# Linear attention: softmaxes of one batch beside the transposes and products of the batch in front of it

## The chip, the cores and the metric

The kernel runs on one NeuronCore of one Trainium2 chip. The metric is the device time of one execution in microseconds (us), as the median of several runs. TensorE (PE) does the matrix products and the transposes, VectorE (DVE) and ScalarE (ACT) work elementwise, GpSimd (POOL) has no work in the stage in question, and the queue of SyncE (SP) issues the DMAs. The engines run apart from each other and wait for each other on semaphores only. Each engine executes its own instructions in the order in which they are written.

## The reference

The program runs four layers on an input of 4 batches x 1024 rows x 512 columns: softmax attention, linear attention, and two state space layers. The change touches the linear attention alone, which is this part of the second layer (16 heads of 32 columns; `mask` hides key rows):

```
    k = jnp.where(mask, -jnp.inf, k)
    v = jnp.where(mask, 0.0, v)
    ...
    q = jax.nn.softmax(q, axis=-1)          # over the 32 columns of a head
    k = jax.nn.softmax(k, axis=2)           # over the 1024 rows of a batch
    attn = jnp.einsum('bhse,bhsd->bhed', k, v)
    y = jnp.einsum('bhtd,bhed->bhte', q, attn)
```

The projections before it have written k transposed (`kT`), q, and v (already masked) to device memory. The stage writes `y` back there, and the next projection reads it.

## The kernel before

`linear_attention` is one block between two barriers. For each of the 4 batches it loads 2 MB of `kT`, 0.5 MB of mask, 2 MB of `q` and 2 MB of `v`, all on SP's queue, and then does these steps. The lines are those of the kernel before.

- **Key softmax.** DVE makes the additive mask `mneg` (L946). Four times, once for each 128 columns, DVE adds it to `kT`, writes `ks` and takes the extreme `nmax` (L950), and ACT takes the exponential with a running sum (L980). DVE inverts the sums (L958) and scales `ks` (L961).
- **Query softmax.** DVE takes the maximum of each head `qmax` (L954) and subtracts it (L956), ACT takes the exponential of all of `q` (L983), DVE sums (L964), inverts (L966) and scales (L968).
- **Turning.** PE transposes the keys into 8 PSUM banks (L1001, "k turn" here), and ACT copies them to `kn` (L986). PE transposes the queries into the same 8 banks (L1008, "q turn"), and ACT copies them to `qT` (L989).
- **Products.** PE multiplies `kn` with `v` into bank 0 (L1013, the "at" product); DVE copies the diagonal 32x32 blocks to `at` (L972, four copies of 32 partitions); PE multiplies `qT` with `at` into the 8 banks (L1019, the "y" product); ACT copies them to `y` (L993); SP stores `y` (L924).

DVE, ACT, PE and SP each run a hardware loop over the batches with these steps in that order. There is one buffer of each of `kT`, `ks`, `q`, `v`. All loads count on one semaphore, `kv_in`, and DVE's first instruction of a batch (L946) waits for all four loads of that batch. SP loads the next `kT` when the four L950 are done, the next `q` when the q turn is done, and the next `v` when the at product is done. On DVE the copy to `at` is the last step of a batch, so the masks and maxima of the next batch stand behind it.

Of the kernel before, what the change touches and what calls it, by code (L numbers as in the profile page):

```python
# [19 lines left out]
P = 128  # L20
# [856 lines left out]

def linear_attention(core, ident, io, scr):

    nc = core.nc  # L880
    with ExitStack() as ctx:
        sb, psum = allocator(nc, ctx, "lin")
        kT = sb("kT", [P, KT, T])
        q = sb("q", [P, TT, D])
        v = sb("v", [P, TT, D])
        mi = sb("mi", [P, T], I32)
        mneg = sb("mneg", [P, T])
        ks = sb("ks", [P, KT, T])
        nmax = sb("nmax", [P, KT])
        ksum = sb("ksum", [P, KT])  # L890
        kr = sb("kr", [P, KT])
        kn = sb("kn", [P, TT, D])
        qmax = sb("qmax", [P, TT * H])
        qsum = sb("qsum", [P, TT * H])
        qr = sb("qr", [P, TT * H])
        qT = sb("qT", [P, KT, T])
        at = sb("at", [P, KT, P])
        y = sb("y", [P, TT, D])
        banks = [psum(f"bank{k}", [P, HALF]) for k in range(8)]
        kv_in = core.count("kv_in")  # L900
        chain_v, y_stored = core.vector_step, core.turned_out[0]
        lin = {n: core.count("lin_" + n) for n in ("k_shift", "k_exp", "k_norm", "q_shift", "q_exp", "q_norm",
                                                   "k_turn", "k_copy", "q_turn", "q_copy", "at", "at_copy",
                                                   "y", "y_copy")}
# [3 lines left out]
        @block.sync  # L908
        def _(sp):
            rows = lambda name, b: scr[name][b].rearrange("(k p) d -> p k d", p=P)  # L910

            def load_k(b):
                sp.dma_start(kT[:], scr["kT"][b]).then_inc(kv_in.handle, 16)
                sp.dma_start(mi[:], io["mask1"][bass.ds(b, 1), :].broadcast_to([P, T])).then_inc(kv_in.handle, 16)

            def load_q(b):
                sp.dma_start(q[:], rows("q", b)).then_inc(kv_in.handle, 16)

            def load_v(b):
                sp.dma_start(v[:], rows("v", b)).then_inc(kv_in.handle, 16)  # L920

            def store_y(b):
                w(sp, "y_copy", b * TT + TT)
                sp.dma_start(scr["y"][b].rearrange("(k p) d -> p k d", p=P), y[:]).then_inc(y_stored.handle, 16)  # L924

            load_k(0)
            load_q(0)
            load_v(0)
            with sp.Fori(0, B - 1) as b:

                w(sp, "k_shift", b * KT + KT)
                load_k(b + 1)
                w(sp, "q_turn", b * TT + TT)
                load_q(b + 1)
                w(sp, "at", b + 1)
                load_v(b + 1)
                store_y(b)
            store_y(B - 1)
            sp.wait_ge(y_stored.handle, y_stored.at(B * 16))

        @block.vector
        def _(dve):
            nc.vector.memset(at[:], 0.0)
            with dve.Fori(0, B) as b:
# [3 lines left out]
                core.apart(dve)  # L948
                for kt in range(KT):
                    nc.vector.tensor_tensor_reduce(ks[:, kt], kT[:, kt], mneg[:], -1.0, HUGE, ALU.add, ALU.min,  # L950
                                                   nmax[:, kt:kt + 1]).then_inc(lin["k_shift"].handle, 1)
                qv = q[:].rearrange("p k (h e) -> p (k h) e", e=DH)
                wide = lambda x: x[:].unsqueeze(2).broadcast_to([P, TT * H, DH])
                nc.vector.tensor_reduce(qmax[:], qv, AX.X, ALU.max).then_inc(chain_v.handle, 1)  # L954
                dve.wait_ge(chain_v.handle, chain_v.at(b * 4 + 2))
                nc.vector.tensor_tensor(qv, qv, wide(qmax), ALU.subtract).then_inc(lin["q_shift"].handle, 1)  # L956
                w(dve, "k_exp", b * KT + KT)
                nc.vector.reciprocal(kr[:], ksum[:]).then_inc(chain_v.handle, 1)  # L958
                dve.wait_ge(chain_v.handle, chain_v.at(b * 4 + 3))
                for kt in range(KT):  # L960
                    last = nc.vector.tensor_scalar(ks[:, kt], ks[:, kt], kr[:, kt:kt + 1], None, ALU.mult)  # L961
# [4 lines left out]
                nc.vector.reciprocal(qr[:], qsum[:]).then_inc(lin["q_norm"].handle, 1)  # L966
                w(dve, "q_norm", b * 2 + 1)
                nc.vector.tensor_tensor(qv, qv, wide(qr), ALU.mult).then_inc(lin["q_norm"].handle, 1)  # L968
                w(dve, "at", b + 1)
                for g in range(4):  # L970
                    r = slice(32 * g, 32 * g + 32)
                    last = nc.vector.tensor_copy(at[r, :, r], banks[0][:].rearrange("p (k e) -> p k e", e=P)[r, :, r])  # L972
                last.then_inc(lin["at_copy"].handle, 1)

        @block.scalar
        def _(act):
            with act.Fori(0, B) as b:
                for kt in range(KT):
                    w(act, "k_shift", b * KT + (kt + 1))
                    nc.scalar.activation(ks[:, kt], ks[:, kt], ACT.Exp, bias=nmax[:, kt:kt + 1], scale=-1.0,  # L980
                                         accum_out=ksum[:, kt:kt + 1]).then_inc(lin["k_exp"].handle, 1)
                w(act, "q_shift", b + 1)
                nc.scalar.activation(q[:], q[:], ACT.Exp).then_inc(lin["q_exp"].handle, 1)  # L983
                for t in range(TT):
                    w(act, "k_turn", b * TT + (t + 1))
                    nc.scalar.copy(kn[:, t], banks[t][:]).then_inc(lin["k_copy"].handle, 1)  # L986
                for t in range(TT):
                    w(act, "q_turn", b * TT + (t + 1))
                    nc.scalar.copy(qT[:, t % 4, (t // 4) * HALF:(t // 4 + 1) * HALF], banks[t][:]).then_inc(lin["q_copy"].handle, 1)  # L989
                act.wait_ge(y_stored.handle, y_stored.at(b * 16))  # L990
                for t in range(TT):
                    w(act, "y", b * TT + (t + 1))
                    nc.scalar.copy(y[:, t], banks[t][:]).then_inc(lin["y_copy"].handle, 1)  # L993

        @block.tensor
        def _(pe):
            with pe.Fori(0, B) as b:
                w(pe, "k_norm", b + 1)
                for t in range(TT):
                    for kt in range(KT):  # L1000
                        last = nc.tensor.transpose(banks[t][:, kt * P:(kt + 1) * P], ks[:, kt, t * P:(t + 1) * P], ident[:])  # L1001
                    last.then_inc(lin["k_turn"].handle, 1)
                w(pe, "q_norm", b * 2 + 2)
                w(pe, "k_copy", b * TT + TT)
                for o in range(8):
                    h, kt = o // 4, o % 4
                    for z in range(4):
                        last = nc.tensor.transpose(banks[o][:, z * P:(z + 1) * P], q[:, h * 4 + z, kt * P:(kt + 1) * P], ident[:])  # L1008
                    last.then_inc(lin["q_turn"].handle, 1)
                w(pe, "q_copy", b * TT + TT)  # L1010
                for kt in range(KT):
                    for t in range(TT):
                        last = nc.tensor.matmul(banks[0][:, kt * P:(kt + 1) * P], v[:, t, kt * P:(kt + 1) * P],  # L1013
                                                kn[:, t, kt * P:(kt + 1) * P], start=(t == 0), stop=(t == TT - 1))
                last.then_inc(lin["at"].handle, 1)
                w(pe, "at_copy", b + 1)
                for t in range(TT):
# [5 lines left out]
    kv_in.stage_added(64 * B)  # L1023
# [943 lines left out]
```

## Time and profile before

| what | value |
|---|---|
| median of 3 runs | 7153.99 us (7148.65 to 7154.7) |
| the profiled execution | 7149.81 us |
| its span in the trace | 7147.8 us |
| the linear attention stage in it | first load issued at 2441.51 us, last copy to `y` starts at 2667.78 us |
| one batch in it (start of L946 to the next) | 50.58, 51.04 and 50.85 us |

The trace counts time from the start of the span. A row of the timeline gives the start, the duration, the engine, the line, the operation with output and inputs, how many instructions were merged into the row, and in brackets how long the engine was idle before it and who ended that.
### The profile page before, as it was taken

The page shows a single profiled execution, that of the slowest core. Times are in us where ns is not written, and L with a number is a line of the kernel's source. Part 1 is how long each engine was busy: PE and PEld are TensorE (multiplying, and loading weights), DVE is VectorE, ACT ScalarE, POOL GpSimd, SP SyncE.
Part 4 walks back from the last instruction along what each step waited for, and adds up shares of the span by engine and source line. Part 5 has one row for each costly group of instructions (what it writes and reads, how often), then busy time and mean ns, then how long its engine had stood idle before and what let it go on. Part 6 is the DMA issues. An engine that isn't in the chain of part 4 may idle for free. (4 is left out here: it accounts for less than half of the span.)

```text
span 7147.8 us, 89203 instructions
## 1 busy us (share of the span) xinstructions
PE 5974.3 (84%) x31488; PEld 4032.9 (56%) x31488; DVE 5020.6 (70%) x6369; ACT 4535.2 (63%) x6817; POOL 2482.0 (35%) x1098
## 2 busy tenths in 40 slices
PE   6989999999889757988858888886888768888883
PEld 2448888888634353434356666663344356666662
DVE  2459999999742245454489999994444489999992
ACT  1228888888621142444478999993455489999991
POOL 0000000000000000000079999993000089999993
PEclk9999999999989878999889999998999899999996
DMA  5442222222242244233356665653233456655554
GB/s 196 170 151 60 72 63 72 67 73 60 79 156 97 107 149 179 86 140 131 149 149 158 172 160 159 158 156 102 97 140 121 153 153 162 159 153 155 154 146 169
DMA packets 608855, 935.18 MB, mean 131 GB/s; under 512 B 104984, under 2 KB 252568, under 8 KB 607908
## 3 DMA queue, kind: packets, MB, share of 16 engines
q1 hardware_dynamic: 596964, 904.27, 41.9%
q0 software_dynamic: 5120, 16.78, 0.7%
q10 hardware_dynamic: 6336, 8.52, 0.3%
q8 instruction: 249, 4.08, 0.3%
q14 instruction: 186, 1.52, 0.1%
HBM read 590.40 MB, written 338.98 MB: 130 GB/s over the span
## 5 line engine op out<-in xcount | busy, mean ns | idle before, releaser
L1609 POOL TENSOR_TENSOR scan_hC<-scan_h,scan_Crep 128x1024 f32<-128x1024 f32 x1024 | 2395.2, 2378 | 2866.5 <-DVE scan_h L1776 2839.1
L1720 ACT ACTIVATE scan_a<-scan_dt,scan_A 128x512 f32<-128x512 f32 x2048 | 1368.2, 697 | 89.9 <-DVE scan_h L1776 72.7
L1643 PE MATMUL scan_y<-ident,scan_hC 128*128 128x128 f32 x8192 | 1114.1, 279 | 298.8 <-POOL scan_hC L1609 293.2
L1643 PEld LDWEIGHTS scan_y<-ident,scan_hC 128*128 128x128 f32 x8192 | 903.5, 142 | 687.6 <-POOL scan_hC L1609 639.7
L1776 DVE TENSOR_TENSOR_SCAN scan_h<-scan_a,scan_carry,scan_h 128x512 f32<-128x512 f32 x1024 | 1217.1, 1261 | 21.9 <-ACT scan_a L1720 19.4
L1776 DVE TENSOR_TENSOR_SCAN scan_h<-scan_a,scan_h 128x512 f32<-128x512 f32 x1024 | 1155.3, 1200 | 55.3 <-ACT scan_a L1720 54.9
L1696 ACT COPY scan_h<-scan_drive 128x1024 f32<-128x1024 f32 x1024 | 1041.8, 1017 | 168.9 <-PE scan_drive L1631 157.2
L1631 PE MATMUL scan_drive<-scan_Bd,scan_dT 128*128 128x256 f32 x4096 | 750.8, 305 | 129.9 <-ACT scan_h L1696 79.3
L805 DVE TENSOR_TENSOR att_pTlo<-att_TP,att_pThi 128x512 fp32r<-128x512 f32 x1024 | 658.1, 684 | 128.0 <-ACT att_pThi L843 126.6
L843 ACT CAST att_pThi<-att_TP 128x512 fp32r<-128x512 f32 x1024 | 547.3, 586 | 180.3 <-PE att_TP L738 173.0
L1631 PEld LDWEIGHTS scan_drive<-scan_Bd,scan_dT 128*128 128x128 f32 x4096 | 558.6, 192 | 181.9 <-issue 96.3
L798 DVE CUSTOM_DVE_ANT_0 att_sm<-att_S,att_mneg 128x1024 f32<-128x1024 f32 x512 | 622.1, 1215 | 12.1 <-POOL att_mneg L716 11.9
L858 ACT ACTIVATE att_pr<-att_sm,att_nmax 128x1024 f32<-128x1024 f32 x512 | 593.0, 1158 | 45.7 <-DVE att_nmax L798 45.7
L738 PE MATMUL att_TP<-ident,att_pr 128*128 128x128 f32 x4096 | 565.4, 278 | 25.6 <-DVE att_pTlo L805 25.6
L497 PE MATMUL p_bank<-p_W,p_xT 128*128 128x512 f32 x1280 | 565.0, 597 | 5.3 <-ACT p_xT L395 5.3
L738 PEld LDWEIGHTS att_TP<-ident,att_pr 128*128 128x128 f32 x4096 | 452.2, 141 | 185.0 <-issue 116.0
L746 PE MATMUL att_YT<-att_pThi,att_v 128*64 128x256 f32 x2048 | 538.3, 298 | 0.0
L1669 PE MATMUL scan_O<-scan_Wo,scan_gT 128*128 128x512 f32 x1024 | 531.9, 613 | 5.4 <-ACT scan_gT L1727 5.4
L1205 PE MATMUL ssmin_ring<-ssmin_Wz,ssmin_xT 128*128 128x512 f32 x1024 | 476.9, 614 | 46.9 <-ACT ssmin_zt L1275 46.9
L746 PE MATMUL att_YT<-att_pTlo,att_v 128*64 128x256 f32 x2048 | 496.7, 277 | 0.0
L716 POOL TENSOR_SCALAR att_mneg<-att_mrow 128x1024 f32<-128x1024 f32 x4 | 14.5, 3635 | 1268.0 <-DMA att_mrow<-mask 840.3
L1205 PE MATMUL ssmin_ring<-ssmin_xT,ssmin_Wx 128*128 128x512 f32 x1024 | 453.1, 598 | 0.0
(151 smaller groups left out, 6826.8 us busy)
## 6 DMA issues: line engine op xcount, KB each, us to landing
scan_dT<-scratch_dtuT SPq DMA_DIRECT2D x512, 256.0 KB, 5.5
scratch_dtuT<-ssmin_dT SPq DMA_DIRECT2D x128, 512.0 KB, 2.9
scan_Crep<-scratch_bc SPq DMA_DIRECT2D x64, 1024.0 KB, 9.7
att_q<-scratch_q_split SPq DMA_DIRECT2D x256, 128.0 KB, 3.0
att_k<-scratch_k_split SPq DMA_DIRECT2D x256, 128.0 KB, 3.2
scratch_uD<-ssmin_uD SPq DMA_DIRECT2D x64, 512.0 KB, 4.4
scratch_z<-ssmin_zt SPq DMA_DIRECT2D x128, 256.0 KB, 2.0
scratch_dt<-ssmin_dt SPq DMA_DIRECT2D x64, 512.0 KB, 2.6
```

The costliest lines, as they stand in the source:

```text
L738: last = nc.tensor.transpose(TP[:, m * P:(m + 1) * P], pr[u % 2][:, m * P:(m + 1) * P], ident[:])
L746: last = nc.tensor.matmul(YT[:, pair * 2 % 4:pair * 2 % 4 + 2, :], v[n // 4 % 2][:, m, n % 4, :].bitcast(F32R), pT[part][pair % 2][:, :, m ...
L798: nc.vector.tensor_tensor_reduce(sm[u % 2][:], S[u % 2][:], mneg[b % 2][:], -1.0, HUGE, ALU.add, ALU.min, nmax[u % 2][:]).then_inc(s["shif ...
L805: nc.vector.tensor_tensor(pT[1][u // 2 % 2][:, u % 2, cols_].bitcast(F32R), TP[:, cols_], pT[0][u // 2 % 2][:, u % 2, cols_], ALU.subtract ...
L858: nc.scalar.activation(pr[u % 2][:], sm[u % 2][:], ACT.Exp, bias=nmax[u % 2][:, 0:1], scale=-1.0, accum_out=psums[:, at:at + 1]).then_inc( ...
L1205: last = nc.tensor.matmul(ring[e % 4][:], lhs, rhs, start=(kt == 0), stop=(kt == KT - 1))
L1609: nc.gpsimd.tensor_tensor(hC[k % 2][:], of, Crep[:, 2 * p:2 * p + 2, :], ALU.mult).then_inc(s["scaled"].handle, 1)
L1631: last = nc.tensor.matmul(drive[:, c * TC:(c + 1) * TC, :], dT[j][:, at * P:(at + 1) * P].bitcast(F32R), Bd[th][:, at, :, first:first + GS ...
L1643: last = nc.tensor.matmul(y[j][:, t, :], hC[k % 2][:, i, t * P:(t + 1) * P], ident[:], start=(p == 0 and i == 0 and t == 0), stop=False, i ...
L1696: nc.scalar.copy(h[group % 3][:, :, tt * P:(tt + 1) * P], drive[:].rearrange("p t n -> p n t")).then_inc(s["laid"].handle, 1)
L1720: nc.scalar.activation(a[(2 * k + i) % 3][:], dt[j][:], ACT.Exp, scale=A[:, m, 2 * p + i:2 * p + i + 1]).then_inc(s["decayed"].handle, 1)
L1776: nc.vector.tensor_tensor_scan(of, a[(2 * k + i) % 3][:], of, first, ALU.mult, ALU.add).then_inc(s["scanned"].handle, 1)
```

## The change

The lines below are those of the changed kernel, about 25 further down.

- `ks`, `q` and `v` get two buffers each, batch b uses number b % 2. `kT`, the mask, `kn`, `qT`, `at`, `y` and the 8 banks stay single.
- The one semaphore for loads becomes several: `k_in` (kT and mask), `q_in` and `v_in` (one for each buffer). DVE waits for `k_in` at the mask and for `q_in` before the maximum of `q`; PE waits for `v_in` before the at product.
- SP issues the loads of batches 0 and 1 first, and in step b those of batch b + 2 ahead of the store of `y`.
- ACT does the exponentials of batch b + 1 between the `qT` copies and the `y` copies of batch b.
- DVE does the copy to `at` of batch b - 1 in batch b, behind the inverse of the sums of `q` and in front of the last scaling of `q`.
- PE keeps its order within a batch. Its waits become one for each bank where it waited for all eight (L1023, L1030), and the at product waits for one copy of `qT` only.
- The hardware loops are gone: the code of the four batches stands in a row. The one `sem_inc` of `core.apart` on DVE is gone too.

```
+            def copy_at(b):
+                w(dve, "at", b + 1)
+                if b >= 1:
+                    w(dve, "y", b * TT)
...
                 nc.vector.reciprocal(qr[:], qsum[:]).then_inc(lin["q_norm"].handle, 1)
+                if b >= 1:
+                    copy_at(b - 1)
                 w(dve, "q_norm", b * 2 + 1)
                 nc.vector.tensor_tensor(qv, qv, wide(qr), ALU.mult).then_inc(lin["q_norm"].handle, 1)
-                w(dve, "at", b + 1)
...
+            copy_at(B - 1)
...
+            exponentials(0)
+            for b in range(B):
...
+                if b + 1 < B:
+                    exponentials(b + 1)
+                if b >= 1:
+                    act.wait_ge(y_stored.handle, y_stored.at(b * 16))
                 for t in range(TT):
                     w(act, "y", b * TT + (t + 1))
...
-                dve.wait_ge(kv_in.handle, kv_in.at(b * 64 + 64))
+                dve.wait_ge(k_in.handle, k_in.at(b * 32 + 32))
...
+                dve.wait_ge(q_in[b % 2].handle, q_in[b % 2].at(b // 2 * 16 + 16))
...
             load_v(0)
-            with sp.Fori(0, B - 1) as b:
...
+            load_k(1)
+            load_q(1)
+            load_v(1)
+            for b in range(B):
+                if b + 2 < B:
+                    load_k(b + 2)
+                    load_q(b + 2)
+                    load_v(b + 2)
```

**ACT's order.** Before, these are the last rows of the loop body on ACT: the copies to `kn`, `qT` and `y`, and the branch back to the exponentials.

```order
L986 COPY lin_kn<-lin_bank 128x512
L989 COPY lin_qT<-lin_bank 128x512 x8
L990 ISA
L993 COPY lin_y<-lin_bank 128x512 x8
L977 REGISTER_ALU
L977 COMPARE_AND_BRANCH
```

Now, from the `kn` copies of batch 0 to the exponential of `q` of batch 2:

```order
L1003 COPY lin_kn<-lin_bank 128x512 x8
L1008 COPY lin_qT<-lin_bank 128x512 x8
L992 ACTIVATE lin_ks,lin_ksum<-lin_ks,lin_nmax 128x1024 x4
L995 ACTIVATE lin_q<-lin_q 128x4096
L1015 COPY lin_y<-lin_bank 128x512 x8
L1003 COPY lin_kn<-lin_bank 128x512 x8
L1008 COPY lin_qT<-lin_bank 128x512 x8
L992 ACTIVATE lin_ks,lin_ksum<-lin_ks,lin_nmax 128x1024 x4
L995 ACTIVATE lin_q<-lin_q 128x4096
```

The exponentials of the next batch (L992, L995) have moved in front of the `y` copies of the batch (L1015), and stand behind its `qT` copies (L1008).

**DVE's order.** Before, the end of the loop body on DVE, from the inverse of the sums of `q`:

```order
L966 RECIPROCAL lin_qr<-lin_qsum 128x128
L905 ISA
L968 TENSOR_TENSOR lin_q<-lin_q,lin_qr 128x4096
L972 COPY lin_at<-lin_bank 32x4x32 x4
L944 REGISTER_ALU
L944 COMPARE_AND_BRANCH
```

Now, the end of batch 1 and the start of batch 2, with the semaphores that each row waits for (`lin_q1` and `lin_ks0` are buffers; `lin_bank0` holds the at product of batch 0):

```order
L975 TENSOR_REDUCE lin_qsum<-lin_q1 128x128 [waits lin_q_exp]
L977 RECIPROCAL lin_qr<-lin_qsum 128x128 [waits vector_step]
L947 COPY lin_at<-lin_bank0 32x4x32 [waits lin_at]
L947 COPY lin_at<-lin_bank0 32x4x32 x3
L981 TENSOR_TENSOR lin_q1<-lin_q1,lin_qr 128x4096 [waits lin_q_norm]
L954 TENSOR_SCALAR lin_mneg<-lin_mi 128x1024 [waits input_in0]
L961 ISA lin_ks0,lin_nmax<-lin_kT,lin_mneg 128x1024 [waits lin_k_exp,lin_k_turn,vector_step]
```

The copy to `at` (L947) is that of the batch in front. It stands behind the whole softmax of the next batch but for the last scaling of `q` (L981).

## Rows read from the trace of the kernel before

**Rows 1.** Busy us (x records) of PE, PEld, DVE, ACT, POOL in the second batch.

```profile
2514.60:2565.50 50.90, 27.44 (x194) 26.55 (x193) 27.89 (x23) 22.07 (x33) 0.00 (x0) 0.73 0.48 175
```

**Rows 2.** Waits in the stage: us in total, times, longest.

```profile
DVE lin_at L972 <- PE lin_bank L1013: 58.1, 4, 14.7
DVE lin_mneg L946 <- DMA lin_v<-scratch_v: 43.7, 4, 21.8
```

**Rows 3.** DMA issues at the stage's head (2441.5 to 2464), us to landing.

```profile
lin_q<-scratch_q SPq DMA_DIRECT2D x1, 2048.0 KB, 16.3
lin_mi<-mask SPq DMA_DIRECT2D x1, 512.0 KB, 10.8
```

**Rows 4.** Timeline of the first batch: start, us, engine, line, operation.

```profile
2441.90 0.42 SPq L914 DMA_DIRECT2D lin_mi<-mask  x1
2442.38 0.43 SPq L917 DMA_DIRECT2D lin_q<-scratch_q  x1
...
2464.01 0.69 DVE L946 TENSOR_SCALAR lin_mneg<-lin_mi 128x1024 f32<-128x1024 int32 x1 [21.84 <-DMA lin_v<-scratch_v]
...
2469.48 4.41 DVE L954 TENSOR_REDUCE lin_qmax<-lin_q 128x128 f32<-128x4096 f32 x1
...
2478.38 3.62 ACT L983 ACTIVATE lin_q<-lin_q 128x4096 f32<-128x4096 f32 x1 [7.55 <-DVE lin_q L956]
2478.47 2.74 DVE L961 TENSOR_SCALAR lin_ks<-lin_ks,lin_kr 128x1024 f32<-128x1024 f32 x4
...
2481.27 6.11 PE L1001 MATMUL lin_bank<-ident,lin_ks 128*128 128x128 f32 x32 [43.52 <-DVE lin_ks L961]
2482.03 4.42 DVE L964 TENSOR_REDUCE lin_qsum<-lin_q 128x128 f32<-128x4096 f32 x1 [0.82 <-ACT lin_q L983]
...
2485.83 2.27 ACT L986 COPY lin_kn<-lin_bank 128x512 f32<-128x512 f32 x4 [0.27 <-PE lin_bank L1001]
2486.49 0.95 DVE L966 RECIPROCAL lin_qr<-lin_qsum 128x128 f32<-128x128 f32 x1
2487.48 4.42 DVE L968 TENSOR_TENSOR lin_q<-lin_q,lin_qr 128x4096 f32<-128x4096 f32 x1
...
2492.03 5.85 PE L1008 MATMUL lin_bank<-ident,lin_q 128*128 128x128 f32 x32 [4.65 <-DVE lin_q L968]
...
2496.59 2.05 ACT L989 COPY lin_qT<-lin_bank 128x512 f32<-128x512 f32 x4 [0.27 <-PE lin_bank L1008]
...
2498.70 7.41 PE L1013 MATMUL lin_bank<-lin_kn,lin_v 128*128 128x128 f32 x64 [0.81 <-ACT lin_qT L989]
...
2506.15 1.19 DVE L972 COPY lin_at<-lin_bank 32x128 f32<-32x128 f32 x4 [14.25 <-PE lin_bank L1013]
...
2507.39 7.41 PE L1019 MATMUL lin_bank<-lin_at,lin_qT 128*128 128x128 f32 x64 [1.28 <-DVE lin_at L972]
```

**Rows 5.** Timeline at later batches: DVE's start of batch 2, ACT's last key exponential, the last copy.

```profile
2514.59 0.69 DVE L946 TENSOR_SCALAR lin_mneg<-lin_mi 128x1024 f32<-128x1024 int32 x1 [7.25 <-DMA lin_v<-scratch_v]
...
2622.07 1.15 ACT L980 ACTIVATE lin_ks<-lin_ks,lin_nmax 128x1024 f32<-128x1024 f32 x1
...
2667.78 0.58 ACT L993 COPY lin_y<-lin_bank 128x512 f32<-128x512 f32 x1 [0.31 <-PE lin_bank L1019]
```

**Rows 6.** Granted clock (behind the busy times) at the k turn, and after the y product.

```profile
2481.27:2486.00 4.73, 4.73 (x22) 4.73 (x23) 3.97 (x1) 3.24 (x6) 0.00 (x0) 0.50 0.00 0
2486.00:2487.40 1.40, 1.38 (x12) 1.14 (x10) 1.36 (x2) 1.28 (x3) 0.00 (x0) 0.92 0.00 0
...
2514.80:2516.80 2.00, 0.00 (x1) 0.00 (x0) 1.81 (x4) 0.65 (x2) 0.00 (x0) 1.00 0.13 49
2516.80:2531.80 15.00, 0.00 (x0) 0.00 (x0) 14.92 (x13) 7.45 (x9) 0.00 (x0) 0.50 0.83 308
```

**Rows 7.** The page's head, and the queue that carries the program's code.

```profile
span 7147.8 us, 89203 instructions
...
q8 instruction: 249, 4.08, 0.3%
```

More of the change, by code:

```diff
@@ L882, in linear_attention @@
         sb, psum = allocator(nc, ctx, "lin")
+        two = lambda n, shape: [sb(f"{n}{j}", shape) for j in range(2)]
         kT = sb("kT", [P, KT, T])
[L884 to L896, printed above, removed]
+        ks, q, v = two("ks", [P, KT, T]), two("q", [P, TT, D]), two("v", [P, TT, D])
+        mi, mneg = sb("mi", [P, T], I32), sb("mneg", [P, T])
+        nmax, ksum, kr = sb("nmax", [P, KT]), sb("ksum", [P, KT]), sb("kr", [P, KT])
+        kn, qT, y = sb("kn", [P, TT, D]), sb("qT", [P, KT, T]), sb("y", [P, TT, D])
+        qmax, qsum, qr = (sb(n, [P, TT * H]) for n in ("qmax", "qsum", "qr"))
         at = sb("at", [P, KT, P])
-        y = sb("y", [P, TT, D])
         banks = [psum(f"bank{k}", [P, HALF]) for k in range(8)]
-        kv_in = core.count("kv_in")
         chain_v, y_stored = core.vector_step, core.turned_out[0]
+        k_in, q_in, v_in = core.input_in[0], core.slot_in[0:2], core.slot_in[2:4]
         lin = {n: core.count("lin_" + n) for n in ("k_shift", "k_exp", "k_norm", "q_shift", "q_exp", "q_norm",
@@ L912, in load_k @@
             def load_k(b):
-                sp.dma_start(kT[:], scr["kT"][b]).then_inc(kv_in.handle, 16)
-                sp.dma_start(mi[:], io["mask1"][bass.ds(b, 1), :].broadcast_to([P, T])).then_inc(kv_in.handle, 16)
+                if b >= 1:
+                    w(sp, "k_shift", b * KT)
+                sp.dma_start(kT[:], scr["kT"][b]).then_inc(k_in.handle, 16)
+                sp.dma_start(mi[:], io["mask1"][b:b + 1, :].broadcast_to([P, T])).then_inc(k_in.handle, 16)
             def load_q(b):
-                sp.dma_start(q[:], rows("q", b)).then_inc(kv_in.handle, 16)
+                if b >= 2:
+                    w(sp, "q_turn", (b - 1) * TT)
+                sp.dma_start(q[b % 2][:], rows("q", b)).then_inc(q_in[b % 2].handle, 16)
             def load_v(b):
[L920 to L924, printed above, removed]
+                if b >= 2:
+                    w(sp, "at", b - 1)
+                sp.dma_start(v[b % 2][:], rows("v", b)).then_inc(v_in[b % 2].handle, 16)
             load_k(0)
@@ L928, in _ @@
             load_v(0)
-            with sp.Fori(0, B - 1) as b:
[L931 to L938, printed above, removed]
+            load_k(1)
[6 more added lines that the diff above has]
+                    load_v(b + 2)
+                w(sp, "y_copy", b * TT + TT)
+                sp.dma_start(scr["y"][b].rearrange("(k p) d -> p k d", p=P), y[:]).then_inc(y_stored.handle, 16)
             sp.wait_ge(y_stored.handle, y_stored.at(B * 16))
@@ L942, in _ @@
         def _(dve):
+            wide = lambda x: x[:].unsqueeze(2).broadcast_to([P, TT * H, DH])
+            def copy_at(b):
+                w(dve, "at", b + 1)
+                if b >= 1:
+                    w(dve, "y", b * TT)
+                for g in range(4):
+                    r = slice(32 * g, 32 * g + 32)
+                    last = nc.vector.tensor_copy(at[r, :, r], banks[0][:].rearrange("p (k e) -> p k e", e=P)[r, :, r])
+                last.then_inc(lin["at_copy"].handle, 1)
             nc.vector.memset(at[:], 0.0)
-            with dve.Fori(0, B) as b:
-                dve.wait_ge(kv_in.handle, kv_in.at(b * 64 + 64))
+            for b in range(B):
+                key, query = ks[b % 2], q[b % 2]
+                dve.wait_ge(k_in.handle, k_in.at(b * 32 + 32))
                 nc.vector.tensor_scalar(mneg[:], mi[:], 1.0, -HUGE, ALU.is_equal, ALU.mult).then_inc(chain_v.handle, 1)
                 dve.wait_ge(chain_v.handle, chain_v.at(b * 4 + 1))
-                core.apart(dve)
+                if b >= 2:
+                    w(dve, "k_turn", (b - 1) * TT)
+                if b >= 1:
+                    w(dve, "k_exp", b * KT)
                 for kt in range(KT):
-                    nc.vector.tensor_tensor_reduce(ks[:, kt], kT[:, kt], mneg[:], -1.0, HUGE, ALU.add, ALU.min,
+                    nc.vector.tensor_tensor_reduce(key[:, kt], kT[:, kt], mneg[:], -1.0, HUGE, ALU.add, ALU.min,
                                                    nmax[:, kt:kt + 1]).then_inc(lin["k_shift"].handle, 1)
-                qv = q[:].rearrange("p k (h e) -> p (k h) e", e=DH)
-                wide = lambda x: x[:].unsqueeze(2).broadcast_to([P, TT * H, DH])
+                qv = query[:].rearrange("p k (h e) -> p (k h) e", e=DH)
+                dve.wait_ge(q_in[b % 2].handle, q_in[b % 2].at(b // 2 * 16 + 16))
                 nc.vector.tensor_reduce(qmax[:], qv, AX.X, ALU.max).then_inc(chain_v.handle, 1)
@@ L960, in _ @@
                 for kt in range(KT):
-                    last = nc.vector.tensor_scalar(ks[:, kt], ks[:, kt], kr[:, kt:kt + 1], None, ALU.mult)
+                    last = nc.vector.tensor_scalar(key[:, kt], key[:, kt], kr[:, kt:kt + 1], None, ALU.mult)
                 last.then_inc(lin["k_norm"].handle, 1)
@@ L966, in _ @@
                 nc.vector.reciprocal(qr[:], qsum[:]).then_inc(lin["q_norm"].handle, 1)
+                if b >= 1:
+                    copy_at(b - 1)
                 w(dve, "q_norm", b * 2 + 1)
                 nc.vector.tensor_tensor(qv, qv, wide(qr), ALU.mult).then_inc(lin["q_norm"].handle, 1)
-                w(dve, "at", b + 1)
-                for g in range(4):
-                    r = slice(32 * g, 32 * g + 32)
-                    last = nc.vector.tensor_copy(at[r, :, r], banks[0][:].rearrange("p (k e) -> p k e", e=P)[r, :, r])
@@ L973, in _, with exponentials @@
-                last.then_inc(lin["at_copy"].handle, 1)
+            copy_at(B - 1)
         @block.scalar
         def _(act):
-            with act.Fori(0, B) as b:
+            def exponentials(b):
+                key, query = ks[b % 2], q[b % 2]
                 for kt in range(KT):
                     w(act, "k_shift", b * KT + (kt + 1))
-                    nc.scalar.activation(ks[:, kt], ks[:, kt], ACT.Exp, bias=nmax[:, kt:kt + 1], scale=-1.0,
+                    if b >= 1 and kt == 0:
+                        w(act, "k_norm", b)
+                    nc.scalar.activation(key[:, kt], key[:, kt], ACT.Exp, bias=nmax[:, kt:kt + 1], scale=-1.0,
@@ L981, in _ @@
                                          accum_out=ksum[:, kt:kt + 1]).then_inc(lin["k_exp"].handle, 1)
                 w(act, "q_shift", b + 1)
-                nc.scalar.activation(q[:], q[:], ACT.Exp).then_inc(lin["q_exp"].handle, 1)
+                nc.scalar.activation(query[:], query[:], ACT.Exp).then_inc(lin["q_exp"].handle, 1)
+            exponentials(0)
+            for b in range(B):
                 for t in range(TT):
                     w(act, "k_turn", b * TT + (t + 1))
+                    if b >= 1 and t == 0:
+                        w(act, "at", b)
@@ L986, in _ @@
                     nc.scalar.copy(kn[:, t], banks[t][:]).then_inc(lin["k_copy"].handle, 1)
[L987 to L990, printed above, removed]
+                for o in range(TT):
+                    w(act, "q_turn", b * TT + (o + 1))
+                    if b >= 1 and o == 0:
+                        w(act, "y", b * TT)
+                    nc.scalar.copy(qT[:, o % 4, (o // 4) * HALF:(o // 4 + 1) * HALF], banks[o][:]).then_inc(lin["q_copy"].handle, 1)
@@ L991, in _ @@
+                if b + 1 < B:
+                    exponentials(b + 1)
+                if b >= 1:
+                    act.wait_ge(y_stored.handle, y_stored.at(b * 16))
                 for t in range(TT):
@@ L996, in _ @@
         def _(pe):
-            with pe.Fori(0, B) as b:
+            for b in range(B):
                 w(pe, "k_norm", b + 1)
                 for t in range(TT):
+                    if b >= 1:
+                        w(pe, "y_copy", (b - 1) * TT + t + 1)
                     for kt in range(KT):
-                        last = nc.tensor.transpose(banks[t][:, kt * P:(kt + 1) * P], ks[:, kt, t * P:(t + 1) * P], ident[:])
+                        last = nc.tensor.transpose(banks[t][:, kt * P:(kt + 1) * P], ks[b % 2][:, kt, t * P:(t + 1) * P], ident[:])
                     last.then_inc(lin["k_turn"].handle, 1)
                 w(pe, "q_norm", b * 2 + 2)
-                w(pe, "k_copy", b * TT + TT)
                 for o in range(8):
                     h, kt = o // 4, o % 4
+                    w(pe, "k_copy", b * TT + o + 1)
                     for z in range(4):
-                        last = nc.tensor.transpose(banks[o][:, z * P:(z + 1) * P], q[:, h * 4 + z, kt * P:(kt + 1) * P], ident[:])
+                        last = nc.tensor.transpose(banks[o][:, z * P:(z + 1) * P], q[b % 2][:, h * 4 + z, kt * P:(kt + 1) * P], ident[:])
                     last.then_inc(lin["q_turn"].handle, 1)
-                w(pe, "q_copy", b * TT + TT)
+                w(pe, "q_copy", b * TT + 1)
+                pe.wait_ge(v_in[b % 2].handle, v_in[b % 2].at(b // 2 * 16 + 16))
                 for kt in range(KT):
                     for t in range(TT):
-                        last = nc.tensor.matmul(banks[0][:, kt * P:(kt + 1) * P], v[:, t, kt * P:(kt + 1) * P],
+                        last = nc.tensor.matmul(banks[0][:, kt * P:(kt + 1) * P], v[b % 2][:, t, kt * P:(kt + 1) * P],
                                                 kn[:, t, kt * P:(kt + 1) * P], start=(t == 0), stop=(t == TT - 1))
@@ L1016, in _ @@
                 w(pe, "at_copy", b + 1)
+                w(pe, "q_copy", b * TT + TT)
                 for t in range(TT):
@@ L1021, in _ @@
                     last.then_inc(lin["y"].handle, 1)
-    kv_in.stage_added(64 * B)
+    k_in.stage_added(32 * B)
+    for j in range(2):
+        q_in[j].stage_added(16 * B // 2)
+        v_in[j].stage_added(16 * B // 2)
     y_stored.stage_added(16 * B)
```

## The prediction, written before the changed kernel ran

> **What bounds the stage now.** I read the windows first. In one batch of 51 us DVE is busy 27.9 us, PE 27.4, ACT 22.1 [rows 1]: no engine is full, so a chain bounds the stage. The waits show how it closes: DVE waits 14 us a batch for the at product before it may copy to `at`, and then 7 us, and at the stage's head 21.8 us, for the load of `v` before the mask [rows 2, 4, 5]. The timeline gives the chain of one batch [rows 4]: key shifts and `q` shift on DVE, exponential of `q`, sums, scaling to 2491.90, q turn, copies to 2498.64, at product, copy to `at`, y product. What could run beside it is held by the one buffer and by the order on the engines. Before the first mask nothing runs but loads.
>
> In this sum I count from DVE's first mask at 2464.01, so the last copy, ending at 2668.36 [rows 5], is at 204.3.
>
> **The head.** The mask lands at 2441.90 + 10.8 = 2452.7, `q` at 2442.38 + 16.3 = 2458.7 [rows 3, 4]; `kT`, issued first, is there before the mask. DVE now needs only these. Mask and shifts take 5.5 us (2464.01 to 2469.48), so they end at 2458.2, and the maximum of `q` starts at 2458.7, where it started at 2469.48. **Gain 10.8 us.** `v` lands at 2464 and is not needed before 2487. The loads of batch 1 are issued at 2458.2; 5 MB queue behind `v`. The head moved 6.7 MB in 22 us, so they need some 16 us and `q` is there by 2480, for a use at about 2486.
>
> **From the first mask to the first copy to `at`.** Batch 0 keeps its times on DVE: the last scaling of `q` ends at 27.9. DVE goes on with batch 1 at once. From its mask to the start of the exponential of `q` it is 14.4 us (2464.01 to 2478.38), so 42.3. ACT has come from the `qT` copies at 34.6 and done the four key exponentials (4 x 1.15 + 0.2 = 4.8, to 39.4), so nothing holds it. From the start of that exponential to the end of the inverse of the sums it is 9.1 us (2478.38 to 2487.48), then the four copies to `at` 1.2 us: 42.3 + 9.1 + 1.2 = 52.6. PE ended the at product at about 41.4, and its y product waits behind the copy until 52.6. Every batch but the last has this new wait on PE; behind it in PE's order stand the transposes of the next batch, and ACT waits for these.
>
> **The period after that.** From one copy to `at` to the next, all on the path:
> - y product 7.41 us at the full clock [rows 4]. PE has idled about 8 us before it. After the y product the row has the clock at 1.00 for 2 us and at 0.50 (1.2 of 2.4 GHz) for the next 15, and the k turn starts at 0.50 for 4.7 us before the clock rises [rows 6]. So I count 4.7 us at half speed, which costs 2.35: 9.8 us. Ends: no cost (7.4), all at half speed (14.8).
> - 16 banks of transposes and their copies. At the full clock the copies set the pace, 2.27 / 4 = 0.57 us a bank, at 0.50 the transposes do (22 in 4.73 us, 0.86 a bank). I take the full clock, as PE comes straight from the y product: 16 x 0.57 = 9.1, and 0.9 until the first copy: 10.0 us. Ends: 9.1 and 14.7.
> - the key exponentials of the next batch, behind the `qT` copies in ACT's order: 4.8 us. DVE has long done their shifts.
> - exponential of `q`, sums, inverse: 9.1 us; copies to `at` 1.2 us.
>
> Sum 9.8 + 10.0 + 4.8 + 9.1 + 1.2 = 34.9 us for a batch, against 51. The at product (7.4 us) ends 8 us before its copy. The scaling of the keys (2.7 us) lies beside the exponential of `q`. The wait of the shifts for the k turn of two batches before, and the wait for the store of `y` (asked for 25 us before it is needed) cost nothing. The second and third copy to `at` end at 87.5 and 122.4.
>
> The Trainium skill, page "TensorE: Matmul & The Clock Gate", section "Loop structure matters more than you think", speaks against this change: a wait of some 8 us in front of matmuls drops the clock and they then run at the low one. The rows agree for such a gap. By the rule the y product pays as above; by its time in the kernel before, where the at product ran just ahead of it, it would not, and the sum would be 7 us lower.
>
> **The last batch.** y product of batch 2 9.8, k and q turn 9.2, at product 7.4, copy 1.2, y product 7.4 (now at full clock), last copy 0.6: 35.6, so the last copy ends at 158.0. That is 46.3 us before 204.3. The store and the barrier behind it are as before.
>
> **Edits at nothing.** The hardware loop: the branch on DVE lies under the wait for `v` [rows 5], on the others under their waits; removed, at most some tenths. The page "Runtime: NRT & Kernel Launch", section "Instruction fetch mechanics", of the Trainium skill says that a taken branch can stall the fetch, which would add to the gain; no row here shows such a stall, so I add nothing. The one buffer of `kT`: its next load is issued when the shifts end, 27 us or more before its use.
>
> **Sum.** 46.3 + 10.8 = 57.1 us. The profiled execution took 7149.8 us (span 7147.8), so 7092.7. It is 4.2 us below the median of the runs; I take half of that on top: **7095 us**.
>
> **Rivals.**
> - *A: PE keeps the full clock at the y product*, as the gap is filled or short. 2.35 us less for three products: 7088. For it: it is 1.00 after the y product for 2 us. Against: it is 0.50 for the 15 us behind those 2 us [rows 6], and the gap is four times as long as they are. Chance 0.08.
> - *B: PE stays at 0.50 nearly throughout.* Period 14.8 + 14.7 + 4.8 + 9.1 + 1.2 = 44.6, last batch 14.8 + 13.8 + 14.8 + 1.2 + 14.8 + 0.6 = 60.0, end at 52.6 + 89.2 + 60.0 = 201.8, a gain of 2.5 + 10.8: 7139. Against: the clock rose after 4.7 us in rows 6, and 27 us of work now come in a row. Chance 0.05.
> - *C: a load comes late.* `q` of batch 2 is asked for at the end of the q turn of batch 0 (34) and lands 9 to 16 us later, by 50; it is needed at 62. The next has about 10 us too. As much again, 10 us in all, would be lost if three 2 MB loads stood ahead of one of them: 7105. Chance 0.06.
> - *D: slower. The straight code arrives late.* A batch is 194 + 193 + 23 + 33 = 443 records [rows 1]; the code queue brought 4.08 MB in 249 packets for 89,203 records [rows 7], so an estimate of 46 to 63 bytes a record gives three more batches 60 to 85 KB, 4 or 5 packets of 16 KB. If each stood behind queued loads as `v` did at the head (21 us) and nothing else ran, it would cost 84 to 105 us: 7095 + 95 = 7190. From 14 us a packet the kernel is slower than before. Against: batch 0, whose code is just as new in a loop, took 50.58 us, where the others took 51.04 and 50.85, and its PE products show no hole. Chance 0.03.
>
> **Numbers.** The forecast has 0.78. Its own range is the unknown size of the clock's cost (-7 to +5 us), handovers and run to run differences (3 runs lie within 6 us): 7084 to 7107; with C the range is 7084 to 7110. A change under 0.2% (14 us) can't be told from none. Faster is the forecast, A and C, and part of B: 0.93. Within 0.2%: the rest of B, 0.04. Slower: D, 0.03.
>
> **What would show it.** The profile of the changed kernel should have DVE's first mask at 2453 and the last `y` copy ending at about 2611; starts of the copies to `at` 35 us apart; a wait of PE for DVE of about 8 us before each y product but the last, and a clock of 0.50 in its first half; the key exponentials of batches 2 and 3 waiting for the copies of `qT` and not for DVE. A period near 33 speaks for A, near 45 for B, a wait of DVE for `q` or `kT` for C, holes in the engines between instructions that wait for nothing for D. The prediction is wrong if the copies to `at` stay 45 us or more apart, or if the stages behind, whose instructions are the same, change by more than 5 us.

## The result and the profile after

The changed kernel takes 7083.22 us (median of 4 runs, 7080.51 to 7086.41) against 7152.1 us for the kernel before (4 runs). The ratio is 0.9904, with a 95% interval of 0.9887 to 0.9921. The forecast was 7095 us in a range of 7084 to 7110: the way was right, and the time lies just under the range. The gain is 69 us, where the sum had 57. The profiled execution took 7080.51 us.

First the head of the stage in the trace after, to be held against [rows 3, 4]. Columns of the timeline: start, duration, engine, line, operation.

```profile
2446.13 0.42 SPq L910 DMA_DIRECT2D lin_mi<-mask  x1
2446.60 0.43 SPq L915 DMA_DIRECT2D lin_q<-scratch_q  x1
...
2455.55 0.69 DVE L954 TENSOR_SCALAR lin_mneg<-lin_mi 128x1024 f32<-128x1024 int32 x1 [9.13 <-DMA lin_mi<-mask]
...
2461.71 4.42 DVE L965 TENSOR_REDUCE lin_qmax<-lin_q 128x128 f32<-128x4096 f32 x1 [0.77 <-DMA lin_q<-scratch_q]
```

DVE now waits 9.1 us for the mask and 0.8 us for `q`, where it waited 21.8 us for `v`. From the first load (2445.76) to the maximum of `q` it is 15.95 us, before it was 27.97: 12.0 us less.

Then one period, from the first copy to `at` to the second. It answers to the batch of [rows 4].

```profile
2508.43 9.55 PE L1045 MATMUL lin_bank<-lin_at,lin_qT 128*128 128x128 f32 x64 [11.03 <-DVE lin_at L947]
...
2517.81 3.66 PE L1025 MATMUL lin_bank<-ident,lin_ks 128*128 128x128 f32 x32
...
2518.49 4.02 ACT L1003 COPY lin_kn<-lin_bank 128x512 f32<-128x512 f32 x8
...
2521.31 3.66 PE L1032 MATMUL lin_bank<-ident,lin_q 128*128 128x128 f32 x32
2522.32 4.13 ACT L1008 COPY lin_qT<-lin_bank 128x512 f32<-128x512 f32 x8
...
2524.80 7.31 PE L1038 MATMUL lin_bank<-lin_kn,lin_v 128*128 128x128 f32 x64
...
2526.14 1.33 ACT L992 ACTIVATE lin_ks<-lin_ks,lin_nmax 128x1024 f32<-128x1024 f32 x1
...
2530.68 3.75 ACT L995 ACTIVATE lin_q<-lin_q 128x4096 f32<-128x4096 f32 x1
2530.95 0.18 DVE L969 RECIPROCAL lin_kr<-lin_ksum 128x4 f32<-128x4 f32 x1 [4.03 <-ACT lin_ks L992]
...
2539.90 1.19 DVE L947 COPY lin_at<-lin_bank 32x128 f32<-32x128 f32 x4
```

The chain is the one that the sum was made of: y product, turns and copies, key exponentials behind the `qT` copies, exponential of `q`, sums, copy to `at`. ACT does the key exponentials right behind the `qT` copies, as forecast for batches 2 and 3, and DVE waits 4.0 us for them. The period is 32.65 us here and 33.4 us in the next, not 34.9.

The clock in it (PEclk, the number behind the five busy times), to be held against [rows 1, 6]: the whole period, the y product's first part, its rest, and the turns.

```profile
core 0: us, PE busy (x) PEld busy (x) DVE busy (x) ACT busy (x) POOL busy (x), PEclk, DMA share, GB/s
2512.75:2545.46 32.71, 23.68 (x194) 23.48 (x194) 27.89 (x24) 20.51 (x34) 0.00 (x0) 0.87 0.75 273
2508.43:2513.00 4.57, 4.57 (x21) 4.57 (x22) 4.57 (x2) 1.17 (x2) 0.00 (x0) 0.51 0.20 72
2513.00:2517.80 4.80, 4.80 (x45) 4.80 (x44) 4.76 (x8) 2.93 (x5) 0.00 (x0) 1.00 0.00 0
2517.81:2525.00 7.19, 7.19 (x68) 7.19 (x67) 7.16 (x4) 6.99 (x15) 0.00 (x0) 1.00 0.78 270
```

DVE's 27.9 us of work in a batch now lie in 32.7 us instead of 50.9. The y product starts at 0.51 for 4.6 us and then has the full clock, and the turns have it throughout. PE's busy time of a batch fell from 27.4 to 23.7 us for the same instructions: the full clock over the turns is a part of the gain.

The end of the stage:

```profile
2597.66 1.19 DVE L947 COPY lin_at<-lin_bank 32x128 f32<-32x128 f32 x4 [18.72 <-PE lin_bank L1038]
2598.90 7.41 PE L1045 MATMUL lin_bank<-lin_at,lin_qT 128*128 128x128 f32 x64 [1.28 <-DVE lin_at L947]
...
2606.34 0.59 ACT L1015 COPY lin_y<-lin_bank 128x512 f32<-128x512 f32 x1 [0.31 <-PE lin_bank L1045]
```

From here on "the stage" is the time from its first load to the end of its last copy to `y`. It is 2606.93 - 2445.76 = 161.2 us after and 2668.36 - 2441.51 = 226.85 us before, so it gained 65.7 us.

### The profile page after: what moved, and what is told of

Same layout as the page of the kernel before. It is cut to its first block and busy times, and to the rows that moved or that the text cites. A ratio compares the mean times of both kernels' runs of the same rounds, so it can differ in the third digit from the quotient of the medians.

```text
span 7078.4 us, 89060 instructions
## 1 busy us (share of the span) xinstructions
PE 5960.9 (84%) x31488; PEld 4016.7 (57%) x31488; DVE 5019.2 (71%) x6369; ACT 4531.9 (64%) x6817; POOL 2480.8 (35%) x1098
## 5 line engine op out<-in xcount | busy, mean ns | idle before, releaser
L1804 DVE TENSOR_TENSOR_SCAN scan_h<-scan_a,scan_carry,scan_h 128x512 f32<-128x512 f32 x1024 | 1216.6, 1258 | 14.1 <-ACT scan_a L1748 10.9
```

The lines of the kernel that those rows point to most:

```text
L1804: nc.vector.tensor_tensor_scan(of, a[(2 * k + i) % 3][:], of, first, ALU.mult, ALU.add).then_inc(s["scanned"].handle, 1)
```

## The experiments

Medians vary by some us, so the table gives the stage in the profiled execution beside them (one trace of each kernel). The kernel before was run beside each: 7158.68 us (13 runs) beside the loops written out, the split semaphores, the old order and PE kept busy; 7157.06 us (11 runs) beside the changed kernel again, the early copy with and without 32 transposes and the q turn; 7155.78 us (7 runs) beside the 58 transposes.

| kernel | median us | ratio to before (95%) | stage us |
|---|---|---|---|
| before | 7155.78 to 7158.68 | | 226.85 |
| loops written out | 7153.25 | 0.9991 (0.9981 to 1.0) | 227.0 |
| and split semaphores | 7114.53 | 0.9949 (0.9932 to 0.9965) | 190.9 |
| two buffers, old order | 7112.96 | 0.9942 (0.9925 to 0.9959) | 187.7 |
| the changed kernel again | 7085.28 | 0.9896 (0.9873 to 0.9918) | 161.4 |
| and PE kept busy | 7078.34 | 0.9895 (0.9878 to 0.9911) | 155.05 |
| copy to `at` earlier | 7071.16 | 0.9877 (0.9855 to 0.99) | 145.2 |
| and 32 transposes | 7070.6 | 0.9878 (0.9854 to 0.9901) | 143.7 |
| and 58 transposes | 7066.58 | 0.9878 (0.986 to 0.9896) | 144.5 |
| loops written out, q turn at full clock | 7140.15 | 0.9975 (0.9962 to 0.9987) | 217.1 |

### Loops written out

```
-            with dve.Fori(0, B) as b:
+            for b in range(B):
```

(the same on ACT and PE, and `B - 1` on SP; ACT's wait for the store of `y` is left out in the first batch)

> The kernel before with its hardware loops in the linear attention written out, nothing else. Theory (the gain is an earlier start and overlap, the loop is free): the same as before within 3 us; three wait gaps of DVE for v of about 7 us stay. Rival (the loop's branches or register arithmetic cost what my sum lacks): 5 to 9 us faster, with batches under 50 us. Rival (straight code arrives late): slower, with holes.

The stage took 227.0 us against 226.85, and its batches 50.8, 52.1 and 51.0 us. DVE's wait for `v` stood as it was:

```profile
DVE lin_mneg L946 <- DMA lin_v<-scratch_v: 43.9, 4, 20.9
```

The median is 5 us lower, 0.1% with an interval that touches 1.0. The stage does not show these 5 us, and I read them as variation; the section on the changed kernel again comes back to them. The loop cost nothing that the stage shows, and straight code brought no holes.

### Split semaphores, one buffer

On top of the written-out loops, with the old order:

```
-                dve.wait_ge(kv_in.handle, kv_in.at(b * 64 + 64))
+                dve.wait_ge(k_in.handle, k_in.at(b * 32 + 32))
...
+                dve.wait_ge(q_in.handle, q_in.at(b * 16 + 16))
                 nc.vector.tensor_reduce(qmax[:], qv, AX.X, ALU.max)...
...
                 w(pe, "q_copy", b * TT + TT)
+                pe.wait_ge(v_in.handle, v_in.at(b * 16 + 16))
```

> Written-out loops and the loads on three semaphores (kT with mask, q, v), still one buffer of each, and the old order on DVE and ACT. Theory: DVE's first maximum of q comes 11 to 12 us earlier, and the three later batches start right behind the copy to at, 7.2 us earlier each: 33 us faster than before, batches of 43.7 us. Rival (the loads then collide with each other, or the exponentials wait for the y copies): only the head, 11 to 15 us faster.

The stage is 36.1 us shorter than with the loops alone, where the theory had 33: 10.9 us in the head, 24.2 from the first maximum of `q` to the fourth, and 1.0 in the last batch. The batches last 43.2, 43.3 and 43.8 us, and the next mask stands right behind the copy to `at`:

```profile
2494.90 1.19 DVE L973 COPY lin_at<-lin_bank 32x128 f32<-32x128 f32 x4 [13.45 <-PE lin_bank L1016]
...
2496.12 0.69 DVE L946 TENSOR_SCALAR lin_mneg<-lin_mi 128x1024 f32<-128x1024 int32 x1
```

More than half of the gain of the whole change needs no second buffer. It comes from waiting for each load at the place of its first use.

### Two buffers, the old order

On DVE the copy goes back to the end of its own batch, on ACT the exponentials of the next batch go behind the `y` copies:

```
                 nc.vector.reciprocal(qr[:], qsum[:]).then_inc(lin["q_norm"].handle, 1)
-                if b >= 1:
-                    copy_at(b - 1)
                 w(dve, "q_norm", b * 2 + 1)
                 nc.vector.tensor_tensor(qv, qv, wide(qr), ALU.mult).then_inc(lin["q_norm"].handle, 1)
-            copy_at(B - 1)
+                copy_at(b)
...
-                if b + 1 < B:
-                    exponentials(b + 1)
...
                     nc.scalar.copy(y[:, t], banks[t][:]).then_inc(lin["y_copy"].handle, 1)
+                if b + 1 < B:
+                    exponentials(b + 1)
```

> The changed kernel with the two order changes undone: the copy to at at the end of its own batch on DVE, the exponentials of the next batch behind the y copies on ACT. Two buffers and earlier loads stay. Theory (two buffers alone are worth nothing, they only permit the order): like the kernel with split semaphores and one buffer, within 3 us, so 33 us faster than before and 35 us slower than the changed kernel; batches of 43.7 us. Rival (the buffers and the earlier loads are a gain of their own): at least 10 us faster than that.

Its stage is 187.7 us, 3.2 us below that of the split semaphores with one buffer and 26.5 us above the changed kernel's, where the expectation had 35. The theory had 33 us for the whole gain over the kernel before and got 39.1, but two buffers by themselves add next to nothing, as it said. The 3.2 us are mostly another edit that this kernel has kept. In the kernel with split semaphores PE waits for all eight `qT` copies before the at product, here for one only, and the bubble of 0.73 to 0.89 us before each of four products is gone. From the start of the q turn to that of the at product it is 2.1 us less in the four batches together, with the clock rising at other moments. The kernel with split semaphores shows the bubble:

```profile
2530.79 7.41 PE L1016 MATMUL lin_bank<-lin_kn,lin_v 128*128 128x128 f32 x64 [0.78 <-ACT lin_qT L990]
```

### PE kept busy before the y product

```
+                w(pe, "q_copy", b * TT + TT)
+                for _ in range(72 if b + 1 < B else 0):
+                    nc.tensor.transpose(banks[7][:, 0:P], ident[:], ident[:])
                 w(pe, "at_copy", b + 1)
-                w(pe, "q_copy", b * TT + TT)
```

> The changed kernel, with 72 transposes of the identity into bank 7 (not read) on PE between the at product and the wait for the copy to at, in the first three batches: the engine is busy for some 8 us of the 9 to 11 us it waited. Theory (the y product costs more there because the clock is at 0.50 when it starts): clock 1.00 in it, 7.4 us in place of 9.4, 10.1 and 8.8, so 6 us faster than the changed kernel, period 31. Rival (the longer y product has another cause, DMA or ACT traffic): its time stays and the kernel is as fast as the changed one or slower.

```profile
2529.95 8.02 PE L1043 MATMUL lin_bank<-ident 128*128 128x128 f32 x72
2537.89 1.19 DVE L947 COPY lin_at<-lin_bank 32x128 f32<-32x128 f32 x4
2539.14 7.41 PE L1047 MATMUL lin_bank<-lin_at,lin_qT 128*128 128x128 f32 x64 [1.17 <-DVE lin_at L947]
```

and the clock from one mask to the next:

```profile
2512.90:2543.40 30.50, 29.34 (x266) 29.10 (x265) 27.83 (x24) 20.44 (x34) 0.00 (x0) 1.00 0.81 293
```

The clock is 1.00 over the whole period, the y product takes 7.41 us, and the stage is 6.1 us shorter, as the theory had it. So the low clock is what the three y products paid for, and 3 x 2.35 = 7.05 us in the sum was near its size.

### The q turn at the full clock in the kernel before

This one measures the term that the sum had wrong. With the loops written out, PE does 32 transposes between the k turn and the q turn:

```
+                w(pe, "k_copy", b * TT + TT)
+                for _ in range(32):
+                    nc.tensor.transpose(banks[7][:, 0:P], ident[:], ident[:])
                 w(pe, "q_norm", b * 2 + 2)
-                w(pe, "k_copy", b * TT + TT)
```

> The kernel before with loops written out, and 32 transposes of the identity into bank 7 (not read) on PE between the k turn and the q turn, where it waited 4 us for the scaling of q. It shows what a bank costs when PE has the full clock from the first. Theory (PE's pace at the full clock is 0.44 us a bank and ACT's 0.50, the 0.57 of my sum still had PE's low clock in it): the q turn spans 3.5 us and its copies 4.1, where they took 5.9 and 5.5, and the stage is 6 to 7 us shorter than with the loops written out alone. Rival (0.57 a bank is ACT's own pace at the full clock, and the changed kernel is faster for another reason): copies 4.6 us, the stage 4 us shorter.

```profile
2493.92 3.71 PE L1006 MATMUL lin_bank<-ident 128*128 128x128 f32 x32 [0.73 <-ACT lin_kn L986]
2497.47 3.66 PE L1011 MATMUL lin_bank<-ident,lin_q 128*128 128x128 f32 x32
2498.11 4.01 ACT L989 COPY lin_qT<-lin_bank 128x512 f32<-128x512 f32 x8 [4.24 <-PE lin_bank L1011]
```

```profile
2493.92:2501.20 7.28, 7.21 (x64) 6.97 (x64) 3.31 (x1) 3.09 (x7) 0.00 (x0) 1.00 0.01 2
```

At a clock of 1.00 the q turn takes 3.66 us (5.85 in the kernel before, 6.26 with the loops written out) and its eight copies 4.01 us: 0.44 us a bank on PE and 0.50 on ACT. The stage is 9.9 us shorter than with the loops alone, more than the 6 to 7 us of the expectation, which had taken the fastest q turn of the kernel before for all four. From the start of the q turn to that of the at product it is 4.71 to 4.76 us here and 6.81 to 7.18 with the loops alone, which makes 9.0 us in four batches. The rival, 0.57 us a bank as ACT's own pace, falls.

### The changed kernel again

> The changed kernel itself once more, beside the kernels of this call. Theory (what the stage does not explain is the variation of the stages that did not change): the linear attention again 161 us from its first load to its last copy, and the stretches before and behind it anywhere within some 10 us of the trace of before. Rival (the change made the stages behind it faster): these again about 8 us shorter than in the kernel before.

The stage took 161.4 us. The stretch from PE's first transpose of the next projection to the end of the span was 4445.8 us here, 4448.4 us in the first trace of the changed kernel, and 4456.3 us in the kernel before. In the others it was 4458.0 (loops written out), 4452.6 (split semaphores), 4447.9 (old order), 4451.1 (PE kept busy), 4450.7 (q turn), 4448.2, 4456.1 and 4447.8 us (the three with the early copy). So the changed kernel was 8 and 10.5 us below the kernel before there. That is the number of the rival, but a kernel with all of the change reached 4456.1. The traces alone can't decide: the four kernels with one buffer lie at 4450.7 to 4458.0 us, and five of the seven traces with two buffers at 4445.8 to 4448.4.

The medians say more. Less the stage of the same kernel's trace they are 6923 to 6926 us for the three kernels with one buffer and written-out loops, and 6922 to 6927 us for the seven results with two buffers. So the buffers and the new order gave nothing outside the stage that can be seen. For the kernel before it is 6925 to 6932 us, and each of the ten is 3 to 9 us below the kernel before that ran beside it. What they all have in common is the written-out loops. Whether some us outside the stage go with them, or the kernel before differs by chance, is not shown.

### The copy to `at` earlier

```
                 last.then_inc(lin["k_norm"].handle, 1)
+                if b >= 1:
+                    copy_at(b - 1)
                 w(dve, "q_exp", b + 1)
                 nc.vector.tensor_reduce(qsum[:], qv, AX.X, ALU.add)...
                 nc.vector.reciprocal(qr[:], qsum[:])...
-                if b >= 1:
-                    copy_at(b - 1)
```

> The changed kernel with the copy to at of the batch in front moved ahead of the sums of q, behind the scaling of the keys. Theory (the period is the chain y product, turns, exponentials, sums, copy; moved, the copy leaves 9 us out of it, until DVE's own work of 28 us a batch bounds): periods 28 us where they were 33, the first copy 6 us earlier, a stage of 145 us, 15 us faster than the changed kernel. Rival (PE or ACT sets the period, or q turn now waits for the later scaling): periods stay above 31, under 8 us faster.

```profile
2501.70 1.18 DVE L947 COPY lin_at<-lin_bank 32x128 f32<-32x128 f32 x4
...
2529.79 1.19 DVE L947 COPY lin_at<-lin_bank 32x128 f32<-32x128 f32 x4
...
2557.87 1.19 DVE L947 COPY lin_at<-lin_bank 32x128 f32<-32x128 f32 x4
```

```profile
2512.70:2540.79 28.09, 23.89 (x201) 23.70 (x200) 27.82 (x24) 21.31 (x35) 0.00 (x0) 0.94 0.87 318
```

The periods are 28.1 us, DVE is busy for 27.8 of 28.1, and the stage is 145.2 us against an expected 145. It is 14.1 us faster than the changed kernel beside it (7071.16 against 7085.28). It beats both kernels, and DVE's own work now bounds the periods.

### The early copy with PE kept busy

The same kernel with 32, then 58 transposes in front of the wait for the copy.

> The kernel with the copy to at moved early, and 32 transposes of the identity into bank 7 (not read) on PE between the at product and the wait for the copy, in three batches. Theory (DVE bounds the periods there, so the clock is worth only the one y product behind the last period): 2 us faster than the kernel without the fill. Rival (the y product is still on the path in every period): 6 us faster.

> As the kernel with the early copy to at and 32 transposes of the identity, but 58 of them, so that PE is busy until the copy in each of the three batches (not read either). With 32, the y product behind the second copy still took 9.04 us and only the last of the three 7.41. Theory (DVE bounds the periods): all three products take 7.4 us, yet the periods stay at 28.1 us and the stage at 143.7, within 0.5 us. Rival (the y product is on the path): periods 26.5, the stage 3 us shorter again.

With 32 the second y product still took 9.04 us (a wait of 3.05 us stood before it) and the third 7.41; the stage was 1.5 us shorter. With 58 all three took 7.3 us, but the transposes ended after the copy and held the product back by 1 to 2 us:

```profile
2497.10 6.50 PE L1043 MATMUL lin_bank<-ident 128*128 128x128 f32 x58
2503.43 7.31 PE L1047 MATMUL lin_bank<-lin_at,lin_qT 128*128 128x128 f32 x64
...
2524.71 6.49 PE L1043 MATMUL lin_bank<-ident 128*128 128x128 f32 x58
2531.04 7.31 PE L1047 MATMUL lin_bank<-lin_at,lin_qT 128*128 128x128 f32 x64
```

In both the periods stayed at 28.1 us: 2 us less in the y product, or a start 1 to 2 us later, no longer move them. The stage of 144.5 us with 58 is within 0.8 us of that with 32, a little outside the 0.5 us of the expectation. The medians of the three kernels with the early copy (7066.6 to 7071.2) can't be told apart.

## Why the prediction was wrong

The chain and every wait in it were right; the sum was 8.6 us short, and the time came out 0.8 us below the range. PE's waits before the three y products were 11.0, 9.0 and 9.0 us, where about 8 were said. Point by point, in the order of the prediction:

- **The head.** Forecast 10.8 us, measured 12.0. The wait moved to the mask and `q` as said. `q` landed 15.1 us after its issue and not 16.3. With the loops alone, where the head is unchanged, it was 15.3 us. So the 1.2 us is how long this one load took in the trace of the kernel before: from the first load to the maximum of `q` it was 27.97 us there, and 27.0 and 26.7 us in the two other kernels with one semaphore.
- **First maximum of `q` to the first y product.** Forecast 47.1 us (52.6 - 5.5), measured 46.7.
- **The y product behind an idle PE.** Forecast 9.8 us, measured 9.4, 10.1 and 8.8. The experiment with PE kept busy gave back the 6 us that it cost. Rival A (the clock stays up) did not come. The rule of the Trainium skill, page "TensorE: Matmul & The Clock Gate", section "Loop structure matters more than you think", held in these rows: after a wait of 11.0 us the y product began at a clock of 0.51.
- **The 16 banks of turns and copies: the step that failed.** The prediction said "At the full clock the copies set the pace, 2.27 / 4 = 0.57 us a bank", and 10.0 us with the start. They take 8.3 us in a period (2517.81 to 2526.14), and 7.0 instead of 9.2 us before the last at product. The row of [rows 4] that I divided, the last four `kn` copies from 2485.83, begins while the clock is still at 0.50 and PE still sets the pace [rows 6]. It mixed PE's slow pace with ACT's, and I took the mean for ACT's own. The right row stood in [rows 4] too: the last four `qT` copies from 2496.59 took 2.05 us, 0.51 a bank, and there the clock is at 1.00 throughout:

```profile
2496.60:2498.70 2.10, 1.28 (x12) 1.05 (x11) 0.00 (x0) 2.05 (x4) 0.00 (x0) 1.00 0.00 0
```

  The experiment at the full clock has 0.50 us a bank for ACT and 0.44 for PE. In the last batch the copies do not set the pace at all: the at product waits for one `qT` copy only, so the 16 banks take PE's own 0.44 us each, 7.0 us. The misread pace is 1.7 us in each of two periods and 2.2 us in the last batch: 5.6 of the missing 8.6 us.
- **The rest.** Key exponentials 4.5 us against 4.8 in each of two periods, the y products 1.1 us in all, the head 1.2, the stretch before the first y product 0.4. Against these, from the exponential of `q` to the end of the copy to `at` it was 10.4 us, not 10.3, in each of two periods.
- **On top of the sum.** Outside the stage the two profiled executions differ by 3.6 us more in favour of the changed kernel (3.7 by their spans): it reached the stage 4.2 us later and took 8.0 us less behind it. The sum had nothing there. The prediction called itself wrong if the stages behind changed by more than 5 us, and by that sign it was; but the stretches and medians of the other kernels show that such differences come without the buffers and the new order. Whether they are chance or go with the written-out loops stays open. The 2.3 us that I added for the median over the profiled execution were right: after, it is 2.7 us. 8.6 and 3.6, less 0.4, are the 11.8 us between 7095 and 7083.2.
- **Rivals B, C, D** did not come: no wait of DVE for a load of a later batch, no holes, no low clock in the turns of a period. D's count of packets was right: with the loops written out, alone or in the changed kernel, the code queue brought 253 packets and not 249, and the stage shows no cost of them. Of D's two figures, 46 and 63 bytes a record, [rows 7] give only the first.
- **The range** allowed 7 us for a cheaper y product, and nothing for the turns being cheaper than a row that was not at the full clock. Their lower end of 9.1 us was the same misread number.

## What to carry to other kernels

A duration that is to hold at another clock must come from a row whose granted clock was that all the way; where a merged row starts in the low stretch, look for another of the same kind (here it stood a few rows further down), or leave a lower end for it. A single semaphore for several loads makes the first use wait for the last load; splitting it was worth 36 of the 66 us with no second buffer. When work is interleaved between batches, look at where the one small step that closes the loop stands in the busiest engine's order: moving the copy to `at` ahead of two long sums was worth another 16 us of the stage.

## What the runs showed of the hardware

- Transposes of 128x128 float32 at a granted clock of 1.00 run at 0.109 us each (3.50 us from the start of one turn of 32 to the next), and at 0.50 at 0.215 us (22 in 4.73 us, [rows 6]). ACT's copies of 512 columns out of PSUM, 0.59 us each on their own, follow one another at 0.49 us when PE is ahead of them ((4.02 - 0.59) / 7).
- Transposes whose result nobody reads kept the clock at 1.00 for what followed: the y product fell from 9.55 to 7.41 us behind 72 of them, and the q turn from 6.26 to 3.66 us behind 32. With waits of 2.71, 1.17 and 1.17 us between the 72 and the product it took 7.41 us each time; behind 32 and a wait of 3.05 us it took 9.04 us.
- Written-out code of four batches in place of a loop made no difference in the stage (227.0 against 226.85 us).
